# Second block's projection: three products of a tile first, then the turning of the tile three back

## What is computed

```python
h = shift_token(x)                       # (2, 1024, 128)
qkv = h @ wqkv                           # 128 x 1536
q, k, v = jnp.split(qkv, 3, axis=-1)     # 8 heads of 64 each
q = l2norm(q) * qs
k = l2norm(k) * ksc
q, k = rotary_xpos(q, k)                 # q*cos*scale + rotate_half(q)*sin*scale
o = local_attention(q, k, v)             # windows of 64, one look back
x = x + o @ wo
```

## Time and profile before

| | us |
|---|---|
| median of three runs | 1209.27 |
| lowest and highest | 1203.18, 1210.47 |
| the profiled execution | 1206.43 |
| its span, first to last instruction | 1204.6 |
| the stage in layer 0, about | 364 to 444 |
| the stage in layer 1, about | 561 to 641 |
| busy over the span: PE, DVE, ACT, POOL | 1074.0, 857.7, 617.3, 516.7 |

### The profile page before, as it was taken

One profiled execution on the slowest core, in us unless ns is written; L12 is line 12 of the kernel. 1 busy time (PEld: TensorE's weight loads), 2 busy tenths in 40 slices (PEclk: granted clock), 3 DMA queues, 4 the chain that ended last, 5 costly groups with the idle time before them and its releaser, 6 DMA issues. The chain is left out here.

```text
span 1204.6 us, 29628 instructions
## 1 busy us (share of the span) xinstructions
PE 1074.0 (89%) x11763; PEld 711.9 (59%) x11763; DVE 857.7 (71%) x1539; ACT 617.3 (51%) x1416; POOL 516.7 (43%) x453
## 2 busy tenths in 40 slices
PE   6799999899998879998888999876998999988998
PEld 4588655688553448655446856533665454444897
DVE  5788567787567978544886835797467589998655
ACT  3566455666445669544668924500664357754000
POOL 1476302667207985322996521033344047742200
PEclk9899999999999989999998999999999989988999
DMA  3200000200002210011220000000000011100011
GB/s 85 82 1 2 8 7 18 82 1 2 1 1 62 61 31 3 2 72 35 55 59 7 3 15 15 13 4 4 4 5 3 15 25 18 18 14 1 14 30 53
DMA packets 52791, 28.08 MB, mean 23 GB/s; under 512 B 35474, under 2 KB 46268, under 8 KB 52284
## 3 DMA queue, kind: packets, MB, share of 16 engines
q1 hardware_dynamic: 52668, 26.36, 8.8%
HBM read 17.17 MB, written 1.05 MB: 15 GB/s over the span
## 5 line engine op out<-in xcount | busy, mean ns | idle before, releaser
L363 POOL TENSOR_TENSOR A_pr<-A_pr,A_rs 128x1024 f32<-128x1024 f32 x64 | 121.1, 1894 | 57.0 <-DVE A_rs L430 57.0
L467 ACT ACTIVATE A_pr<-psb,A_nm 128x1024 f32<-128x1024 f32 x64 | 71.1, 1111 | 49.9 <-DVE A_nm L424 49.6
L420 DVE TENSOR_REDUCE A_mx<-psb 128x1 f32<-128x1024 f32 x64 | 78.1, 1220 | 8.3 <-PE psb L376 4.5
L1280 POOL TENSOR_TENSOR F_raw<-F_raw,F_rc 128x1024 f32<-128x1024 f32 x32 | 75.6, 2364 | 16.5 <-DVE F_raw L1350 16.0
L2116 PE MATMUL psb<-M_wd,M_gates 128*128 128x128 f32 x512 | 70.7, 282 | 0.0
L2050 PE MATMUL psb<-XL,M_wu 128*128 128x512 f32 x128 | 69.3, 624 | 1.2 <-ACT M_ST L2174 1.2
L2116 PEld LDWEIGHTS psb<-M_wd,M_gates 128*128 128x128 f32 x512 | 65.6, 195 | 3.9 <-DVE M_gates L2348 2.1
L2053 PE MATMUL psb<-XL,M_wg 128*128 128x512 f32 x128 | 67.5, 609 | 0.0
L2348 DVE TENSOR_TENSOR M_gates<-M_hall,psb 128x512 f32<-128x512 f32 x64 | 43.9, 687 | 33.1 <-PE psb L2111 33.0
L1298 PE MATMUL psb<-F_wqkv,F_hst 128*128 128x512 f32 x128 | 61.3, 601 | 6.2 <-ACT F_hst L1361 4.5
L389 PE MATMUL psb<-ident,A_pr 128*128 128x128 f32 x512 | 66.6, 285 | 0.0
(11 more groups left out here) (396 smaller groups left out, 2974.8 us busy)
## 6 DMA issues: line engine op xcount, KB each, us to landing
F_VS<-F_V SPq DMA_DIRECT2D x62, 128.0 KB, 2.3
F_raw<-in_c_xpos_dram SPq DMA_DIRECT2D x3, 1024.0 KB, 4.8
F_wqkv<-in_L_ffn_wqkv_dram SPq DMA_DIRECT2D x3, 768.0 KB, 7.3
A_w<-in_L_attn_w_dram SPq DMA_DIRECT2D x4, 256.0 KB, 3.6
M_wu<-in_L_ffn_Wup_dram SPq DMA_DIRECT2D x16, 64.0 KB, 2.0
M_wg<-in_L_ffn_Wgate_dram SPq DMA_DIRECT2D x16, 64.0 KB, 2.1
M_wd<-in_L_ffn_Wdown_dram SPq DMA_DIRECT2D x16, 64.0 KB, 1.7
M_sel<-in_c_select_dram SPq DMA_DIRECT2D x16, 64.0 KB, 1.9
```

Source lines behind the costliest of these rows:

```text
L363: pool.tensor_tensor(p, p, rs[:, u % 2:u % 2 + 1].broadcast_to([P, SEQ]), ALU.mult).then_inc(scaled, 1)
L420: dve.tensor_reduce(mx[:, u % 2:u % 2 + 1], sview(u), AX, ALU.max).then_inc(maxed, 1)
L467: act.activation(pr[:, u % NP, :], sview(u), ACT.Exp, bias=nm[:, u % 2:u % 2 + 1], scale=scale, accum_out=su[:, u % 2:u % 2 + 1]).then_inc ...
L1280: pool.tensor_tensor(rs[:, o, :], rs[:, o, :], rc[:, o, :], ALU.add).then_inc(unit, 1)
```

## The change

`make` is split: it keeps the q and k products and signals a new semaphore, `paired`; the v product becomes `value`, which signals `made`. PE's order becomes make(n), value(n), turn(n-3), and the first six tiles and the last turnings are written out accordingly. ACT's square waits for `paired`, and its copy of the value for `made`. ACT's copy of a turned tile is that of n-3 and goes ahead of the square root. DVE's wait for POOL's finish of tile n-2 goes behind the sum of squares. The waits for `roped` in `make` and for `turned` in `rope` stay as they are.

```diff
                                 for i in range(2):
-                                    pe.matmul(bank[2 * o + i], hst[:, o, :], F_wqkv[:, i * HD:(i + 1) * HD], start=True, stop=True)
+                                    last = pe.matmul(bank[2 * o + i], hst[:, o, :], F_wqkv[:, i * HD:(i + 1) * HD], start=True, stop=True)
+                                last.then_inc(paired, 1)
+
+                            def value(n, o, first):
                                 if not (first and o == 0):
                                     pe.wait_ge(v_kept, n)
                                 pe.matmul(bank[4], hst[:, o, :], F_wqkv[:, 2 * HD:3 * HD], start=True, stop=True).then_inc(made, 1)
...
                             make(0, 0, True)
+                            value(0, 0, True)
                             make(1, 1, True)
-                            for o in range(2):
-                                make(2 + o, o, False)
-                                turn(o, o, True)
-                            with pe.Fori(2, HT) as i:
+                            value(1, 1, True)
+                            make(2, 0, False)
+                            value(2, 0, False)
+                            make(3, 1, False)
+                            value(3, 1, False)
+                            turn(0, 0, True)
...
+                            with pe.Fori(3, HT) as i:
                                 for o in range(2):
                                     make(2 * i + o, o, False)
-                                    turn(2 * i + o - 2, o, False)
+                                    value(2 * i + o, o, False)
+                                    turn(2 * i + o - 3, 1 - o, False)
+                            turn(NT - 3, 1, False)
...
                                 dve.wait_ge(squared, n + 1)
-                                if not first:
-                                    dve.wait_ge(unit, 2 * n - 2)
...
                                 step(dve.tensor_reduce(sums, sq[:, o, :].rearrange("p (h d) -> p h d", d=DH), AX, ALU.add))
+                                if not first:
+                                    dve.wait_ge(unit, 2 * n - 2)
...
-                            def tile(n, o, first, last):
-                                act.wait_ge(made, n + 1)
+                            def tile(n, o, first, last, kept=None):
+                                act.wait_ge(paired, n + 1)
...
+                                act.wait_ge(made, n + 1)
                                 act.activation(V[:, ds(n, 1), :, :].rearrange("p o h d -> p (o h d)"), bank[4], ACT.Copy).then_inc(v_kept, 1)
                                 if not last:
                                     stage(n + 2, o)
+                                if kept is not None:
+                                    keep(kept)
                                 act.wait_ge(summed, n + 1)
```

More of the change, by code:

```diff
@@ L1245, in build @@
                     VS = sb("F_VS", [P, NT, HEADS, DH], stack=sa)
-                    g = (loaded, zeroed, staged, made, squared, v_kept, summed, rooted, inv, roped, unit, turned, q_kept, k_kept,
-                         dstep, v_moved) = sems("F1", "loaded zeroed staged made squared v_kept summed rooted inv roped unit "
+                    g = (loaded, zeroed, staged, paired, made, squared, v_kept, summed, rooted, inv, roped, unit, turned, q_kept, k_kept,
+                         dstep, v_moved) = sems("F1", "loaded zeroed staged paired made squared v_kept summed rooted inv roped unit "
                                                 "turned q_kept k_kept dstep v_moved", st)
@@ L1311, in multiply @@
                             make(0, 0, True)
+                            value(0, 0, True)
                             make(1, 1, True)
-                            for o in range(2):
-                                make(2 + o, o, False)
-                                turn(o, o, True)
-                            with pe.Fori(2, HT) as i:
+                            value(1, 1, True)
[4 more added lines that the diff above has]
+                            turn(0, 0, True)
+                            make(4, 0, False)
+                            value(4, 0, False)
+                            turn(1, 1, True)
+                            make(5, 1, False)
+                            value(5, 1, False)
+                            turn(2, 0, False)
+                            with pe.Fori(3, HT) as i:
                                 for o in range(2):
                                     make(2 * i + o, o, False)
-                                    turn(2 * i + o - 2, o, False)
+                                    value(2 * i + o, o, False)
+                                    turn(2 * i + o - 3, 1 - o, False)
+                            turn(NT - 3, 1, False)
                             for o in range(2):
@@ L1381, in activate @@
                                 tile(o, o, True, False)
-                            for o in range(2):
-                                tile(2 + o, o, False, False)
-                                keep(o)
+                            tile(2, 0, False, False)
+                            tile(3, 1, False, False, 0)
                             with act.Fori(2, HT - 1) as i:
                                 for o in range(2):
-                                    tile(2 * i + o, o, False, False)
-                                    keep(2 * i + o - 2)
+                                    tile(2 * i + o, o, False, False, 2 * i + o - 3)
                             for o in range(2):
-                                tile(NT - 2 + o, o, False, True)
-                                keep(NT - 4 + o)
+                                tile(NT - 2 + o, o, False, True, NT - 5 + o)
+                            keep(NT - 3)
                             keep(NT - 2)
```

## The result

The changed kernel takes 1224.64 us (median of four runs, 1224.43 to 1226.68) against 1207.05 for the kernel before (four runs), a ratio of 1.014 with a 95% interval of 1.011 to 1.017. It is slower by 17.6 us; 1224 had been forecast. The profiled execution took 1226.68 us, span 1224.8.

The account below looks back on a forecast made before the run. POOL was taken to bound the kernel before, a ring of PE and DVE after: 5.15 us per tile, 7.43 us more in layer 0 and 8.22 in layer 1, together 15.7, giving 1222.1 to 1225.0; forecast 1224, range 1215 to 1232.

Parts of the forecast that it names:

- part (b): Turning three back: PE and DVE strictly in turn, 5.15 us per tile, above POOL's 4.30.
- Part (a): ACT's square waits for two products, not three: starts 0.86 us earlier per layer at the entrance, hidden in the steady part.
- (c): ACT's copy of the turned tile ahead of the square root: the root is not late, the extra wait costs nothing.
- (d): DVE's wait for POOL's finish behind the reduce: had held the reduce once, for 0.4 us; expected to change nothing.
- the hand-off from PE to DVE: Delay from the end of the transposes on PE to DVE's last two rope products, put at 0.04 us per tile.
- the hand-off to PE: Delay from DVE's last rope product to PE's next make, put at 0.06 us per tile.
- the load and six passes: PE's exposed first weight load, 0.11 us, and the six passes of make and value, 2.58 us, per tile.
- my 15.7: Forecast loss in us over both layers, from the turning of tile 14 coming 7.43 and 8.22 later.
- the ring: Closed round turn(n-3), DVE's last two rope products, make(n+1), value(n+1), turn(n-2): 5.15 us per tile, ends 4.94 and 5.35.
- POOL without gaps: First rival: ring does not bind, POOL does tiles at 4.30 us; 5.4 us less, 1204; chance 0.05.
- The shorter ring: Second rival: drain of the transposes overlapped, 4.75 us per tile, 6.1 us more in all, 1215; chance 0.10.
- the lower clock: Third rival: PE's idle time in each round brings 1.2 GHz; 1312, or 1233 with a tenth of rounds hit; chance 0.04.

## Why the prediction was right

The mechanism was that of part (b), and each sign named there is in the trace: PE idle ahead of the first product (1.49 us, 1.4 forecast), nothing ahead of the transposes, POOL idle 0.87 to 0.89 us a tile (0.85 forecast), L1364 behind the last transpose. Part (a), the earlier square: the first square starts 2.08 us after its first product (364.11 to 366.19) and did 2.94 before, the 0.86 forecast. Parts (c) and (d) were costed at nothing. (c) is right for the changed kernel, where the copy stands ahead of the root; I had looked at whether the copy delays the root, while the runs show the other side, that a copy behind the root delays the next turning by 0.15 us a tile, and at the end of the stage makes PE wait 4.26 us in place of 1.27. I did not see that this part of the change avoids that. (d) was not run by itself and rests on the trace alone: in it the maximum never waits long enough to appear among the waits of the changed kernel.

One term was mis-sized: the hand-off from PE to DVE, put at 0.04 from the earlier trace rows and measured at 0.14 in the loop. The transposes were 1.04 (1.09 forecast, their first weight load being hidden behind the value product), the rope 1.29 (1.27), the hand-off to PE 0.05 (0.06), the load and six passes 2.68 (2.69). Together 5.20 against 5.15. Over 24 rounds the measured 5.21 gives 15.7 + 1.5, or 17.2 us; 17.6 was measured. The forecast of 1224 lay on the point because I added my 15.7 to a base of 1208.3, between the profiled execution and the median of the runs then shown (1209.27), and the median of before with a run more is 1207.05: a difference too small by 1.9 and a base too high by 1.3. That the total agrees so closely is luck; that the ring is right is not.

Of the rivals, POOL without gaps came true only where the ring was opened, in three different ways, at 1202 each time; its time had been worked out as 1204, or 5.4 us less than before, and the version two back is 5.4 us below the kernel before. The shorter ring and the lower clock are excluded for the changed kernel by the 5.21 us and by the granted clock of 1.00. The Trainium skill, in "TensorE: Matmul & The Clock Gate", section "HAM oscillation — how this bites in real kernels", describes a loop whose waits between bursts of matmuls bring the clock down before each burst; the waits of that loop are longer than those of this ring, so its account does not speak for the third rival. The trace agrees: waits of 1.5 us in every 5.2 left the granted clock at 1.00. Two places where it was 0.50 had longer waits of PE ahead of them: 2.23 us in the fill of layer 0 of the kernel before (though after the same wait in layer 1 it was 1.00), and 4.26 us at the end of the stage in the run with the turning alone moved.

The version that turns two back and lets the square wait for two products is faster than both kernels, 1202 against 1207 and 1225; the one with the value product behind the turning and the one with three buffers can't be told from it. All three have POOL's adds 4.30 to 4.32 us apart on average, so POOL's work is likely to be the next bound; no run tests that.

## What to carry to other kernels

Before moving a step in an in-order queue, write down for each buffer who waits for whom, and go round: if the step that frees a buffer stands directly ahead of the step that needs what the buffer releases, the engines take turns, and the period is the sum of their work however idle each one is. The cure is to put independent work of the first engine between the two, to keep the old distance, or to add a buffer; each of them brought the time to 1202 us here. A dose of extra work tells how many tiles the ring spans that sets the pace: of a dose in it, the share that shows per tile is one over that number, here one and a third.

## What the runs showed of the hardware

A product that in a loop needs a register operation for its addresses started 0.10 us later after its wait was met than the same product with the loop written out (0.14 against 0.03 us). The loops of all engines were written out at once, so that it is this operation rests on the trace alone. Where a wait closes a ring the delay is paid in every round: 2.4 us over 24 rounds by the spacing of the adds. The medians differ by 3.0 us, or by 2.0 when each is taken against the kernel before on its own chip.

Waits of 1.5 us of PE in every 5.2 left the granted clock at 1.00 all along the changed stage; behind a wait of 2.23 us in the kernel before it was 0.50 in layer 0 and 1.00 in layer 1.
